# Last layer of a four-layer image kernel: both images stacked in the operand rows of the transforms

## The chip, the cores and the metric

The kernel runs on one core of one Trainium2 chip. The metric is the device time of one execution in microseconds.

## The reference

An activation of shape (2, 96, 48, 48) (two images, 96 channels) goes through four layers; each computes its result from the group-normalised x and adds it to x. The change is in the last one:

```python
x_0, x_05, x_1 = x[:, :32], x[:, 32:64], x[:, 64:]          # 32 channels each
x_0   = 3x3 convolution of x_0, weights gated per image
Fre   = Fh @ fftshift(x_05) @ Fw                            # fractional Fourier matrices, complex, per image
Mix   = gated 1x1 convolution of [Fre.real, Fre.imag]       # 64 -> 64, per image, plus bias
IFRFT = abs(Fh(-alpha) @ complex(Mix) @ Fw(-alpha)) / (H * W)
fre   = rfft2(x_1)
mix   = gated 1x1 convolution of [fre.real, fre.imag]       # 64 -> 64, per image, plus bias
x_1   = irfft2(complex(mix))
out   = 3x3 convolution of concatenate([x_0, IFRFT, x_1]) + bias
x     = x + out
```

H = W = 48; an rfft row has UH = 25 values. A fractional matrix is E diag(phase) E^T, with a real E of 48x48 and a phase that depends on the image's alpha.

## The kernel before, in words

The program is a list of blocks, one after another; a block ends when all five engines have met. The last layer (`l3`) is `group_norm`, `l3_gates`, `l3_forward`, `l3_inverse`. TensorE (PE) computes `lhsT^T @ rhs` from SBUF into one of eight PSUM banks; ScalarE (ACT) or VectorE (DVE) copies a bank out; SyncE (SP) issues every DMA; GpSimd (POOL) only clears tiles. An f32 matmul of the program is two PE instructions in the trace.

`l3_gates` computes the gates and the mixing weights `wg`, and loads `xh` (the image rows on 48 partitions), the tables, and `G0`, the shifted input of the first convolution.

`l3_forward` has four phases on TensorE, each a list of jobs of one PSUM bank; ACT copies every bank out (L1753, L1755), and a phase waits for the copies of the one before.
1. Rows (`rows_jobs`): for each of the BC = 64 image-channel pairs one matmul with the 48x48 `xh` of that pair as the stationary operand, 48 moving columns (`ef`) for the fractional part and 96 (`fh`) for the Fourier part. Result: `A1`, `A2` on 48 partitions.
2. Columns (`cols_jobs`): for each of the 48 rows j one matmul of `A1[:, :, j]` (48 rows, 64 weight columns) by `ef`, and two by `fw`, 50 columns each. Result on the 64 pairs: `Xh`, `Fz`. DVE multiplies `Xh` by the phases into `Zr` and `Zi`.
3. Fractional mixing (`frac_jobs`): per chunk of ten rows (FCH, five chunks) and per result (real, imaginary) three accumulating matmuls of 480 columns: `wg` of the real part, of the imaginary part (64 rows each), and a one-row matmul with the bias.
4. Fourier mixing (`mix_jobs`): the same with chunks of 250 columns.

```python
yield ([(wg[:, 0, 0, q, :], Zr[:, lo:hi, :].rearrange("p j k -> p (j k)"), 0, o, True, False),
        (wg[:, 0, 1, q, :], Zi[:, lo:hi, :].rearrange("p j k -> p (j k)"), 0, o, False, False),
        (bw[:, 0, q, :], e11[:, lo * H:hi * H], 0, o, False, True)], BC,
```

DVE turns the mixed values by the phases again (L1779 to L1783), and SP stores them to DRAM as `V` (L1670) and the Fourier part as `M` (L1672).

`l3_inverse` loads `Mu` and `Vj` from DRAM with the row index on 48 partitions (L1852, L1857). TensorE does the first convolution (`conv0_jobs`, 96 rows, 32 output rows), then kind 1 and 2 (inverse Fourier, `Mu` by `ih`, `A4` by `iw`) into `F`, then kind 3 and 4 (`Vj` by `ei`, `A3` by `ei`, squared by ACT). DVE adds the squares into `P2`, ACT takes the root. SP carries `F` and `P2` through DRAM into `cat`, channels on partitions (L1859 to L1870): `F` while kind 3 and 4 run, `P2` per image. The last convolution (L1912, nine taps of 384 columns, twelve banks) waits for `F` and, per image, for that image's `P2`. The order of the queues is the order of the statements in each engine's function.

## Time and profile before

| | us |
|---|---|
| median of 3 runs | 3371.29 (3369.62 to 3373.77) |
| profiled execution, its own time | 3376.56 |
| its span in the trace | 3374.7 |
| last layer from its gates to the end | 3003.3 to 3374.7 |
| forward block | 3034.9 to 3183.6 |
| inverse block up to the last convolution | 3183.6 to 3293.0 |
| last convolution | 3293.0 to 3366.4 |
| PE busy in the whole span | 67% |
| mean granted clock of TensorE | 0.853 |

In a table by stage each row is a stretch of the span: how long each engine was busy in it and with how many instructions, and the clock that TensorE was granted, as a share of 2.4 GHz (0.50 is 1.2 GHz). A group of instructions gives the busy time, the mean duration of one (for PE with its latency, so that instructions overlap), and the idle time before them. L12 is line 12 of the kernel; the lines of the changed kernel are its own.

### The profile page before, as it was taken

The page shows a single profiled execution, that of the slowest core. Times are in us where ns is not written, and L with a number is a line of the kernel's source. Part 1 is how long each engine was busy: PE and PEld are TensorE (multiplying, and loading weights), DVE is VectorE, ACT ScalarE, POOL GpSimd, SP SyncE. Part 2 cuts the span into 40 slices and gives each one's busy share as a digit, 9 for nine tenths or more (in the row PEclk, how much of TensorE's full clock was granted, in tenths as well). Part 3 has the DMA queues.
Part 4 walks back from the last instruction along what each step waited for, and adds up shares of the span by engine and source line. Part 5 has one row for each costly group of instructions (what it writes and reads, how often), then busy time and mean ns, then how long its engine had stood idle before and what let it go on. Part 6 is the DMA issues. An engine that isn't in the chain of part 4 may idle for free. (4 is left out here: it accounts for less than half of the span.)

```text
span 3374.7 us, 25934 instructions
## 1 busy us (share of the span) xinstructions
PE 2266.1 (67%) x7808; PEld 1113.2 (33%) x7808; DVE 2652.9 (79%) x2063; ACT 1636.3 (48%) x2346; POOL 2126.1 (63%) x1108
## 2 busy tenths in 40 slices
PE   4554466666666666666666664885079886939998
PEld 1221133233332332323223231322034443517294
DVE  7676799999999999999999997669556668952101
ACT  4454577767677767766777673253100006502130
POOL 4165799999999999999999995045300006910000
PEclk8766799999999999999999998766589898965659
DMA  1176434333443443433344335000387951040411
GB/s 42 59 219 216 132 121 128 120 111 121 133 122 114 117 127 123 127 113 123 122 127 122 109 124 201 35 0 0 91 301 264 322 205 37 12 59 1 47 19 32
DMA packets 156204, 387.94 MB, mean 115 GB/s; under 512 B 56883, under 2 KB 65367, under 8 KB 142647
## 3 DMA queue, kind: packets, MB, share of 16 engines
q1 hardware_dynamic: 150342, 368.07, 36.0%
q10 hardware_dynamic: 5730, 18.29, 1.5%
q8 instruction: 61, 1.00, 0.1%
q14 instruction: 71, 0.58, 0.1%
HBM read 311.32 MB, written 61.61 MB: 111 GB/s over the span
## 5 line engine op out<-in xcount | busy, mean ns | idle before, releaser
L811 POOL TENSOR_TENSOR l0c_r<-l0c_r,l0c_v 128x768 f32<-128x768 f32 x576 | 1041.0, 1823 | 23.7 <-DVE l0c_r L774 22.6
L839 ACT ACTIVATE ps<-l0c_dlt,l0c_na 128x512 f32<-128x512 f32 (+1 forms) x1152 | 625.9, 575 | 515.8 <-DVE l0c_h L800 492.0
L800 DVE TENSOR_TENSOR_SCAN l0c_h<-ps,l0c_h,l0c_r 128x768 f32<-128x768 f32 x384 | 703.4, 1832 | 5.0 <-issue 5.0
L820 POOL TENSOR_TENSOR l0c_hcp<-l0c_cb,l0c_h 128x768 f32<-128x768 f32 x384 | 699.8, 1822 | 0.6 <-DVE l0c_h L800 0.6
L864 ACT ACTIVATE l0c_r<-l0c_S,l0c_floor,l0c_na 128x768 f32<-128x768 f32 x576 | 583.6, 1014 | 14.2 <-ACT l0c_y L832 14.2
L704 PE MATMUL ps<-l0c_Bp,l0c_sel 96*128 96x512 bf16 (+1 forms) x1152 | 294.2, 338 | 439.2 <-DVE l0c_hcv L781 258.7
L737 PE MATMUL ps<-l0c_hcp,net_ident 128*128 128x512 f32 (+1 forms) x1536 | 582.8, 503 | 9.0 <-ACT l0c_y L832 6.0
L774 DVE SCALAR_TENSOR_TENSOR l0c_r<-l0c_r,ps 128x768 f32<-128x768 f32 x576 | 547.6, 951 | 6.4 <-PE ps L704 3.8
L737 PEld LDWEIGHTS ps<-l0c_hcp,net_ident 128*128 128x128 f32 x1536 | 270.3, 196 | 256.2 <-issue 199.3
L1297 PE MATMUL ps<-l_prod,l_wa 128*96 128x384 f32 (+1 forms) x888 | 292.1, 493 | 88.7 <-DVE l_prod L1281 88.7
L800 DVE TENSOR_TENSOR_SCAN l0c_h<-ps,l0c_r 128x768 f32<-128x768 f32 x192 | 339.4, 1768 | 0.0
L1281 DVE TENSOR_TENSOR l_prod<-l_base,l_other 128x2304 f32<-128x2304 f32 (+1 forms) x74 | 189.3, 2558 | 141.3 <-PE ps L1297 88.9
L737 PE MATMUL ps<-l0c_hcv,net_ident 128*128 128x512 f32 (+1 forms) x768 | 289.8, 500 | 1.1
L704 PEld LDWEIGHTS ps<-l0c_Bp,l0c_sel 96*128 96x128 bf16 x1152 | 85.7, 98 | 618.5 <-DVE l0c_r L774 529.0
L1378 POOL MEMSET l2g_pad<- 96x224 f32 x4 | 1.1, 281 | 363.0 <-POOLq L116 363.0
L1297 PEld LDWEIGHTS ps<-l_prod,l_wa 128*96 128x96 f32 (+1 forms) x888 | 146.7, 165 | 233.6 <-issue 144.2
L704 PE MATMUL ps<-l0c_Cp,l0c_sel 96*128 96x256 bf16 (+1 forms) x384 | 96.1, 332 | 157.8 <-DVE l0c_r L774 156.2
L162 ACT ACTIVATE net_rstd<-gn_t 96x2 f32<-96x2 f32 x4 | 0.8, 203 | 413.2 <-DVE gn_t L141 413.2
L1187 POOL TENSOR_TENSOR l_Z<-l_Z,l0f_prod 128x2304 f32<-128x2304 f32 x13 | 85.1, 6556 | 183.3 <-ACT l0f_prod L1108 182.7
L781 DVE TENSOR_TENSOR l0c_hcv<-ps,l0c_h 128x768 f32<-128x768 f32 x192 | 186.6, 972 | 0.0
L1493 PE MATMUL ps<-l_rows,l_diag 128*128 128x384 f32 x450 | 153.7, 504 | 34.8 <-ACT l_diag L1399 19.3
L737 PEld LDWEIGHTS ps<-l0c_hcv,net_ident 128*128 128x128 f32 x768 | 134.4, 195 | 124.4 <-issue 98.6
(261 smaller groups left out, 2821.6 us busy)
## 6 DMA issues: line engine op xcount, KB each, us to landing
l0c_cb<-cf SPq DMA_DIRECT2D x768, 192.0 KB, 3.4
l_other<-po SPq DMA_DIRECT2D x72, 1152.0 KB, 5.2
dlt<-l0s_dl SPq DMA_DIRECT2D x36, 384.0 KB, 3.5
v<-l0s_vv SPq DMA_DIRECT2D x36, 384.0 KB, 2.3
...
```

The costliest lines, as they stand in the source:

```text
L704: mm = pe.matmul(ps[:, lo:hi], sel[:, t % 2, n * 128:(n + 1) * 128], rows[:, i, lo - at:hi - at], start=True, stop=True)
L737: mm = pe.matmul(ps[:, lo:hi], ident[:, :], hc[:, lo - PY:hi - PY], start=(n == 0), stop=(n == N - 1))
L774: dve.scalar_tensor_tensor(rj, rj, 1.0, b_all, ALU.add, ALU.mult).then_inc(s_ub, 1)
L781: dve.tensor_tensor(hcv[:, dve_steps(j) % NHV, :], c_all, h[:, j % N, :], ALU.mult).then_inc(s_hv, 1)
L800: dve.tensor_tensor_scan(h[:, n, :], da[j % 2], r[:, j % NR, :], init, ALU.mult, ALU.add).then_inc(s_scan, 1)
L811: pool.tensor_tensor(r[:, j % NR, :], r[:, j % NR, :], v[:, (j // N) % 2, :], ALU.mult).then_inc(s_w, 1)
L820: pool.tensor_tensor(hcp[:, p % NHP, :], cb[:, p % NCB, :], h[:, e % N, :], ALU.mult).then_inc(s_hp, 1)
L839: act.activation(da[e % 2][:, part], dlt[:, i, part], ACT.Exp, scale=na[:, i, n:n + 1]).then_inc(done, 1)
L864: act.activation(r[:, j % NR, :], S[:, i, :], ACT.Tanh, bias=floor[:, :], scale=na[:, i, N + n:N + n + 1]).then_inc(s_tanh, 1)
L1281: dve.tensor_tensor(prod[0:n, s, :], base[0:n, s, :], other[0:n, s, :], ALU.mult).then_inc(s_prod, 1)
L1297: mm = pe.matmul(ps[0:C, c * BANK:c * BANK + CH], wa[0:height[i], i, :], prod[0:height[i], i % 3, c * CH:(c + 1) * CH], start=(i == 0), st ...
L1493: mm = pe.matmul(ps[:, o:o + CH], diag[:, tl, i, :], rows[:, tl, dy + 8 * c:dy + 8 * c + 8, dx:dx + W], start=(i == 0), stop=(i == NPE - 1))
```

## The change

Both images, or the real and the imaginary part, share one matmul:
- `xh` holds both images on 96 partitions. The row tables are block matrices: `ef2` is `ef` twice on the diagonal (96x96), `fh2` 96x192. One matmul per channel gives both images, side by side in the columns.
- `A1` and `A2` have 128 partitions; POOL clears them and the upper 80 stay zero; `ef` and `fw` are padded with zero rows to 128. The column matmuls are issued twice (q = 0, 1), into the lower and the upper 64 rows of a bank: the upper half repeats the real columns for the fractional part, and for the Fourier part the lower half gets the real 25 and the upper half the imaginary 25 columns. So the real and imaginary parts are stacked on 128 partitions.
- The phases are taken by DVE: `PZ`, `PA`, `PB` are 128x2304 tables computed at the block's start (three passes each). DVE reads the real columns from PSUM, multiplies by `PZ` into `Z`; after the mixing it reads two banks, multiplies them by `PA` and `PB`, adds, and SP stores that chunk of `V`.
- Mixing is one matmul of 128 rows with `wg` (real and imaginary results as 128 columns), a second with `ws` (the same weights, swapped and negated) for the turned product, each with a one-row matmul for the bias in the fractional part; in the Fourier part the bias goes into ACT's copy. Chunks there are of 20 rows (500 columns).
- The inverse does the first convolution, then the fractional part (`Vj`, `A3` by `ei2`, a block matrix), then the Fourier part (`Mu` by `ih2`, copied out by DVE, then `A4` by `iw2`), each with both images in 96 or 100 rows. `P2` and `F` have 96 partitions.
- SP loads `V` before `M`, in four gathers each. It then sends `P2` in two halves of 16 channels and `F` in four chunks of 8, each by a store to DRAM, a wait for its landing and two gathers into `cat`; the last convolution waits for all of them.
- POOL clears only the borders of `G0` and `cat`.

```diff
+            for name in ("ef2", "fh2", "ef", "fw"):
+                sp.dma_start(tr[name][tuple(slice(None) for _ in tr[name].shape)], a[name]).then_inc(s_tr, 16)
...
+            pool.memset(tr["A1"][:, :, :, :], 0.0).then_inc(s_pad, 1)
+            pool.memset(tr["A2"][:, :, :, :, :], 0.0).then_inc(s_pad, 1)
...
+            for p, b, rows in groups:
+                step(dve.tensor_tensor(wg[rows, :, :, b, :], gate[rows, :, :].rearrange("p f (q o) -> p f q o", q=2),
+                                       wt[rows, :, :].rearrange("p f (q o) -> p f q o", q=2), ALU.mult))
...
+            step(dve.tensor_scalar(ws[:, 0, :, :], wg[:, 0, 1, :, :], -1.0, None, ALU.mult))
+            step(dve.tensor_scalar(ws[:, 1, :, :], wg[:, 0, 0, :, :], 1.0, None, ALU.mult))
...
+            for i, (lo, hi) in enumerate(FCH):
                 sp.wait_ge(s_v, i + 1)
-                sp.dma_start(d["V"][:, i, :, :], M[:, i, :, :]).then_inc(s_out, 16)
-            sp.wait_ge(s_m, 1)
-            sp.dma_start(d["M"].rearrange("p u i k -> p (u i k)"), Mz[:, :, :, :].rearrange("p u i k -> p (u i k)")
-                         ).then_inc(s_mst, 16)
+                sp.dma_start(d["V"][:, lo:hi, :], V[:, lo:hi, :]).then_inc(s_vst, 16)
...
-            for lo, hi in FCH:
-                yield ([(A1[:, :, j], ef[:, :], (j - lo) * H, H, True, True) for j in range(lo, hi)], BC,
...
-                    mms.append((A2[:, :, 0, u], fw[:, 0, :], (u - lo) * 2 * UH, 2 * UH, True, False))
-                    mms.append((A2[:, :, 1, u], fw[:, 1, :], (u - lo) * 2 * UH, 2 * UH, False, True))
...
-                    yield ([(wg[:, 0, 0, q, :], Zr[:, lo:hi, :].rearrange("p j k -> p (j k)"), 0, o, True, False),
-                            (wg[:, 0, 1, q, :], Zi[:, lo:hi, :].rearrange("p j k -> p (j k)"), 0, o, False, False),
-                            (bw[:, 0, q, :], e11[:, lo * H:hi * H], 0, o, False, True)], BC,
...
+            for i, (lo, hi) in enumerate(R0):
+                free(q_r0 + i)
+                for c in range(lo, hi):
+                    o = (q_r0 + i) % 8 * BANK + (c - lo) * 2 * H
+                    mm = pe.matmul(ps[0:W, o:o + 2 * H], xh[:, 0, c, :], ef2[:, :], start=True, stop=True)
+                mm.then_inc(s_mm, 1)
...
+                    mm = pe.matmul(ps[0:W, o:o + 4 * H], xh[:, 1, c, :], fh2[:, :], start=True, stop=True)
...
+            for i, (lo, hi) in enumerate(FCH):
+                free(q_c0 + i)
+                for j in range(lo, hi):
+                    o = (q_c0 + i) % 8 * BANK + (j - lo) * H
+                    for q in range(2):
+                        mm = pe.matmul(ps[BC * q:BC * q + BC, o:o + H], A1[:, :, :, j].rearrange("p b c -> p (b c)"),
+                                       ef[:, :], start=True, stop=True)
+                mm.then_inc(s_mm, 1)
...
+                for u in range(lo, hi):
+                    o = (q_c1 + i) % 8 * BANK + (u - lo) * UH
+                    for q in range(2):
+                        for s in range(2):
+                            mm = pe.matmul(ps[BC * q:BC * q + BC, o:o + UH],
+                                           A2[:, :, :, s, u].rearrange("p b c -> p (b c)"),
+                                           fw[:, s, UH * q:UH * q + UH], start=(s == 0), stop=(s == 1))
...
+                for w, b, q in ((wg[:, 0, :, :, :], bw, q_fr + 2 * i), (ws[:, :, :, :], bws, q_fr + 2 * i + 1)):
+                    free(q)
+                    pe.matmul(ps[:, bank(q, n)], w.rearrange("p q b o -> p (q b o)"),
+                              Z[:, lo:hi, :].rearrange("p j k -> p (j k)"), start=True, stop=False)
+                    pe.matmul(ps[:, bank(q, n)], b[:, :, :].rearrange("p q n -> p (q n)"), e11[:, lo * H:hi * H],
+                              start=False, stop=True).then_inc(s_mm, 1)
...
+                pe.matmul(ps[:, bank(q_mx + i, (hi - lo) * UH)], wg[:, 1, :, :, :].rearrange("p q b o -> p (q b o)"),
+                          Fz[:, lo:hi, :].rearrange("p u k -> p (u k)"), start=True, stop=True).then_inc(s_mm, 1)
...
+            phase(PZ, csz, 1, ALU.subtract)
+            phase(PA, cs, 1, ALU.subtract)
...
+                dve.scalar_tensor_tensor(Z[:, lo:hi, :].rearrange("p j k -> p (j k)"),
+                                         ps[:, bank(q_c0 + i, (hi - lo) * H)], float(H),
+                                         PZ[:, lo:hi, :].rearrange("p j k -> p (j k)"), ALU.mult, ALU.mult
+                                         ).then_inc(s_ed, 1)
+            phase(PB, cs, 0, ALU.add)
...
+                for k, (dst, P, done) in enumerate(((v1, PA, s_m1), (v2, PB, s_m2))):
+                    q = q_fr + 2 * i + k
+                    dve.wait_ge(s_mm, q + 1)
+                    dve.tensor_tensor(dst[:, s, 0:n], ps[:, bank(q, n)], P[:, lo:hi, :].rearrange("p j k -> p (j k)"),
+                                      ALU.mult).then_inc(s_ed, 1)
+                dve.wait_ge(s_ed, evac_count(q_fr + 2 * i + 1))
+                dve.tensor_tensor(V[:, lo:hi, :].rearrange("p j k -> p (j k)"), v1[:, s, 0:n], v2[:, s, 0:n], ALU.add
...
+                    sp.dma_start(Vj[H * b:H * b + H, :, s, :], d["V"][o:o + C3, :, :].rearrange("c j k -> j c k")
+                                 ).then_inc(s_V, 16)
...
-            sp.wait_ge(s_ev, first[3])
-            sp.dma_start(d["o"][1], F[:, :, :]).then_inc(s_fst, 16)
-            sp.wait_ge(s_edge, 1)
-            sp.wait_ge(s_fst, 16)
             for b in range(B):
-                sp.dma_start(interior(cat[2 * C3:C, b, :, :]),
-                             d["o"][1, :, C3 * b:C3 * b + C3, :].rearrange("h c w -> c h w")).then_inc(s_cf, 16)
-            for b in range(B):
-                rows = slice(C3 * b, C3 * b + C3)
-                sp.wait_ge(s_root, b + 1)
-                sp.dma_start(d["o"][0][:, rows, :], P2[:, rows, :]).then_inc(s_pst, 16)
-                sp.wait_ge(s_pst, 16 * (b + 1))
-                sp.dma_start(interior(cat[C3:2 * C3, b, :, :]),
-                             d["o"][0, :, rows, :].rearrange("h c w -> c h w")).then_inc(s_cp[b], 16)
...
+            def to_cat(i, lo, hi):
+                for b in range(B):
+                    r0 = C3 * (2 if i else 1)
+                    sp.dma_start(interior(cat[r0 + lo:r0 + hi, b, :, :]),
+                                 d["o"][i, H * b:H * b + H, lo:hi, :].rearrange("h c w -> c h w")).then_inc(s_cat, 16)
+
+            for g in range(2):
+                lo, hi = HALF * g, HALF * (g + 1)
+                sp.wait_ge(s_root, g + 1)
+                sp.dma_start(d["o"][0, :, lo:hi, :], P2[:, lo:hi, :]).then_inc(s_pst, 16)
+                sp.wait_ge(s_pst, 16 * (g + 1))
+                to_cat(0, lo, hi)
+            for i, (lo, hi) in enumerate(K2):
+                sp.wait_ge(s_ea, evac_count(q_2 + i))
+                sp.dma_start(d["o"][1, :, 2 * lo:2 * hi, :], F[:, 2 * lo:2 * hi, :]).then_inc(s_fst, 16)
+                sp.wait_ge(s_fst, 16 * (i + 1))
+                to_cat(1, 2 * lo, 2 * hi)
...
+                    mm = pe.matmul(ps[0:D2, o:o + D2], Vj[:, c, :, :].rearrange("p q k -> p (q k)"), ei2[:, :],
+                                   start=True, stop=True)
...
+                    mm = pe.matmul(ps[0:D2, o:o + D2], A3[:, c, :], ei2[:, :], start=True, stop=True)
...
+                    mm = pe.matmul(ps[0:Q2, o:o + 2 * D2], Mu[:, 2 * c:2 * c + 2, :, :].rearrange("p c q k -> p (c q k)"),
+                                   ih2[:, :], start=True, stop=True)
...
+                        mm = pe.matmul(ps[0:D2, o:o + 2 * W], A4[:, c, s, :], iw2[:, s, :],
+                                       start=(s == 0), stop=(s == 1))
...
+            pe.wait_ge(s_cat, 16 * B * (2 + len(K2)))
...
+    def blocks(m):
+
+        r, n = m.shape
+        two = np.zeros((2, r, 2, n), f)
+        two[0, :, 0], two[1, :, 1] = m, m
+        return two.reshape(2 * r, 2 * n)
```

How the queues are changed, at three places. First TensorE in the forward block, before (`ps` is PSUM, `l3w_xbuf` is `xh`, `l3f_A` is `A1` and `A2`; the figures are output rows by moving columns; one row is one matmul of the program):

```order
L1737 MATMUL ps<-l3w_ef,l3w_xbuf 48x48 x64
L1737 MATMUL ps<-l3w_fh,l3w_xbuf 48x96 x64
L1737 MATMUL ps<-l3w_ef,l3f_A 64x48 x48
L1737 MATMUL ps<-l3w_fw,l3f_A 64x50 x96
L1737 MATMUL ps<-l3f_Zr,l3w_wg 64x480
L1737 MATMUL ps<-l3f_Zi,l3w_wg 64x480
L1737 MATMUL ps<-l3f_e,l3w_bw 64x480
```

and now:

```order
L1722 MATMUL ps<-l3w_ef,l3w_xh 48x96 x32
L1728 MATMUL ps<-l3w_fh,l3w_xh 48x192 x32
L1736 MATMUL ps<-l3w_ef,l3w_A 64x48 x96
L1746 MATMUL ps<-l3w_fw,l3w_A 64x25 x192
L1756 MATMUL ps<-l3f_Z,l3w_wg 128x480
L1758 MATMUL ps<-l3f_e,l3w_bw 128x480
L1756 MATMUL ps<-l3f_Z,l3w_ws 128x480
L1758 MATMUL ps<-l3f_e,l3w_bws 128x480
```

The 64 row matmuls of either kind became 32 with twice the columns, the column matmuls 96 of 48 and 192 of 25 columns, and the mixing has two matmuls per result in place of three.

Second, TensorE in the inverse block before:

```order
L1901 MATMUL ps<-l_G,l_w0g 32x384 x36
L1901 MATMUL ps<-l3i_ih,l3i_Mu 50x96 x64
L1901 MATMUL ps<-l3i_iw,l3i_A 48x48 x128
L1901 MATMUL ps<-l3i_ei,l3i_Vj 48x48 x128
L1901 MATMUL ps<-l3i_ei,l3i_A 48x48 x128
L1912 MATMUL ps<-l3i_cat,l3i_w 96x384 x108
```

and now:

```order
L1935 MATMUL ps<-l_G,l_w0g 32x384 x36
L1944 MATMUL ps<-l3i_ei,l3i_Vj 96x96 x32
L1952 MATMUL ps<-l3i_ei,l3i_A 96x96 x32
L1959 MATMUL ps<-l3i_ih,l3i_Mu 100x192 x16
L1968 MATMUL ps<-l3i_iw,l3i_A 96x96 x32
L1977 MATMUL ps<-l3i_cat,l3i_w 96x384 x108
```

The fractional stages moved ahead of the Fourier stages, and each of the four has a quarter of the matmuls, of twice the width.

Third, SyncE in the inverse block behind the loads, before (`o` is the scratch in DRAM):

```order
L1859 DMA o<-l3i_F 48x3072
L1863 DMA l3i_cat<-o 32x48x48 x2
L1868 DMA o<-l3i_P 48x1536
L1870 DMA l3i_cat<-o 32x48x48
L1868 DMA o<-l3i_P 48x1536
L1870 DMA l3i_cat<-o 32x48x48
```

and now, the first three of six such trips:

```order
L1904 DMA o<-l3i_P 96x768
L1898 DMA l3i_cat<-o 16x48x48 x2
L1904 DMA o<-l3i_P 96x768
L1898 DMA l3i_cat<-o 16x48x48 x2
L1909 DMA o<-l3i_F 96x384
L1898 DMA l3i_cat<-o 8x48x48 x2
```

What was one trip for `F`, issued ahead of everything, and one per image for `P2` is now two trips for `P2` and then four for `F` in one queue.

## Rows read from the trace of the kernel before

**Rows 1.** Chain of waits, 2880 to 3375 us: start, us, what.
```profile
by line: PE ps L1901 21.3%; PE ps L1912 14.6%; issue 0.6%; ACT l3i_A L1937 0.2%; DVE net_X L1955 0.1%
...
3290.34 2.70 issue
3293.04 72.47 PE ps L1912 x216
```

**Rows 2.** By stage: length; busy us (instructions) per engine; granted clock; DMA share, GB/s.
```profile
core 0: us, PE busy (x) PEld busy (x) DVE busy (x) ACT busy (x) POOL busy (x), PEclk, DMA share, GB/s
3003.30:3034.90 31.60, 6.47 (x42) 2.68 (x42) 4.29 (x22) 4.38 (x9) 4.09 (x1) 0.50 1.07 138
3034.90:3045.80 10.90, 10.19 (x127) 10.19 (x128) 10.59 (x6) 3.08 (x6) 0.00 (x0) 0.50 0.02 4
3045.80:3067.10 21.30, 20.76 (x132) 20.44 (x130) 5.05 (x2) 7.64 (x15) 0.00 (x0) 0.50 0.00 1
3067.10:3077.70 10.60, 10.57 (x96) 10.58 (x97) 0.00 (x0) 2.26 (x4) 0.00 (x0) 0.50 0.00 0
3077.70:3099.70 22.00, 21.49 (x195) 21.32 (x193) 5.02 (x2) 3.23 (x6) 0.00 (x0) 0.50 0.01 1
3099.70:3150.20 50.50, 49.88 (x60) 10.19 (x60) 0.01 (x1) 5.37 (x11) 0.00 (x0) 0.50 0.00 0
3150.20:3178.50 28.30, 27.80 (x60) 10.12 (x60) 15.21 (x6) 3.67 (x11) 0.00 (x0) 0.50 0.20 42
3178.50:3183.60 5.10, 0.00 (x0) 0.00 (x0) 0.00 (x0) 0.10 (x1) 0.00 (x0) 0.50 0.57 120
```

**Rows 3.** The same, around changes of clock, and in an earlier layer.
```profile
3183.60:3189.00 5.40, 5.33 (x9) 1.60 (x10) 0.00 (x0) 0.57 (x1) 4.26 (x1) 0.50 0.90 91
3189.00:3209.60 20.60, 20.60 (x64) 6.82 (x62) 0.00 (x0) 5.75 (x10) 0.00 (x0) 1.00 1.00 82
3209.60:3212.90 3.30, 3.30 (x41) 3.28 (x41) 0.00 (x0) 2.27 (x4) 0.00 (x0) 1.00 0.02 5
3212.90:3293.00 80.10, 76.29 (x859) 75.65 (x857) 3.50 (x2) 26.66 (x46) 0.00 (x0) 0.50 0.15 23
3293.00:3298.20 5.20, 5.16 (x8) 2.38 (x9) 0.00 (x0) 1.16 (x1) 0.00 (x0) 0.50 0.26 57
...
2184.00:2232.00 48.00, 44.33 (x58) 14.39 (x57) 32.51 (x27) 16.03 (x21) 0.00 (x0) 0.50 0.00 1
```

**Rows 4.** Groups of PE matmuls, one line: busy us, mean ns | idle before.
```profile
L222 PE MATMUL ps<-l0x_XG,l0p_w_in 96*128 96x384 f32 x48 | 21.2, 603 | 11.4 <-DMA l0p_cb<-in_cb 7.8 <-ACT l0p_pad L240 3.7
...
L222 PE MATMUL ps<-l0x_XG,l0p_w_in 96*64 96x384 f32 x48 | 12.1, 663 | 12.8 <-ACT l_Z L238 12.8
```

**Rows 5.** Groups of ACT and DVE.
```profile
L1755 ACT COPY l3f_A<-ps 48x480 f32<-48x480 f32 x18 | 9.9, 552 | 35.2 <-PE ps L1737 35.2
...
L1768 DVE TENSOR_TENSOR l3f_Zi<-l3w_cs 64x2304 f32<-64x2304 f32 x1 | 2.6, 2551 | 0.0
...
L774 DVE SCALAR_TENSOR_TENSOR l0c_r<-l0c_r,ps 128x768 f32<-128x768 f32 x576 | 547.6, 951 | 6.4 <-PE ps L704 3.8
...
L1923 ACT ACTIVATE l3i_P<-l3i_P 48x1536 f32<-48x1536 f32 x2 | 3.0, 1483 | 1.8 <-DVE l3i_P L1948 1.8
...
L1923 ACT ACT_TABLE_LOAD x1 | 1.3, 1283 | 0.0
```

**Rows 6.** SyncE: an issue, landings of L1857, landings by tile (KB, median us).
```profile
3253.98 0.99 SPq L1863 DMA_DIRECT2D l3i_cat<-o  x2
...
DMA to landing us min/median/max: 11.1/13.3/15.6
...
l3i_cat<-o SPq DMA_DIRECT2D x4, 288.0 KB, 3.9
...
o<-l3i_F SPq DMA_DIRECT2D x1, 576.0 KB, 5.0
o<-l3i_P SPq DMA_DIRECT2D x2, 288.0 KB, 3.1
...
l_back<-l_acc SPq DMA_DIRECT2D x1, 144.0 KB, 2.4
```

More of the change, by code:

```diff
@@ new lines, in l3_inverse, with by_dve, evac_count, bank @@
+        q_3 = B * NC
+        q_4 = q_3 + len(K3)
+        q_1 = q_4 + len(K3)
+        q_2 = q_1 + len(K1)
+        q_c = q_2 + len(K2)
+        HALF = C3 // 2
+        half_done = [next(i for i, (lo, hi) in enumerate(K3) if hi >= HALF * (g + 1)) for g in range(2)]
+        def by_dve(q):
+            return q_1 <= q < q_2
+        def evac_count(q):
+            return sum(by_dve(i) == by_dve(q) for i in range(q + 1))
+        def bank(q, n):
+            return slice(q % 8 * BANK, q % 8 * BANK + n)
@@ L1905, in _ @@
[L1905 to L1916 removed]
+                    pe.wait_ge(s_ed if by_dve(q - 8) else s_ea, evac_count(q - 8))
@@ L1918, in _ @@
+            for n in range(B * NC):
+                b, c = divmod(n, NC)
+                free(q_c + n)
+                for i in range(TAPS):
+                    dy, dx = divmod(i, 3)
+                    mm = pe.matmul(ps[0:C, bank(q_c + n, CH)], w2[:, i, :],
+                                   cat[:, b, dy + 8 * c:dy + 8 * c + 8, dx:dx + W], start=(i == 0),
+                                   stop=(i == TAPS - 1))
+                mm.then_inc(s_c2, 1)
         @block.scalar
         def _(act):
-            def root(b):
-                rows = slice(C3 * b, C3 * b + C3)
-                act.wait_ge(s_sum, b + 1)
-                act.activation(P2[:, rows, :], P2[:, rows, :], ACT.Sqrt, scale=1.0 / (H * W)).then_inc(s_root, 1)
```

541 lines of the change are left out of this document (265 added, 276 removed).

## The prediction

> **What bounds the kernel now.** I read the page's chain of waits first: its last stretch is PE alone, lines L1901 and L1912, with almost no other engine [rows 1]. So in the last layer TensorE's own time is the path. The table by stage then shows which part of that is what: from 3034.9 to 3178.5 us the forward block keeps PE busy all through [rows 2], and of the inverse the same holds (76 of 80 us [rows 3]). The reader is to see two things in it. The stages cost what their streamed columns cost (10.9, 21.3, 10.6, 22.0, 50.5 and 28.3 us), and the granted clock is 0.50 in every one, which is the 1.2 GHz level. The third view is the clock around the changes of shape [rows 3]. The first convolution (L1901 on l_G, operands of 96 rows) starts at 0.50 and is at 1.00 (2.4 GHz) 5.4 us later; it holds that for 20.6 us. Then the 48-row stage begins, still at 1.00, and 3.3 us later the clock is 0.50 and stays there for 80 us although PE is busy 76 of them. The last convolution, 96 rows again, is at 1.00 after 5.2 us. In a much earlier layer 48 us of almost full PE, on alternating operands of 128, 64 and 2 rows, ran at 0.50. What went before each rise was therefore continuous work of 96 or more rows, what went before the fall was continuous work of 48. This is what the change can move: it brings nearly every operand to 96, 100 or 128 rows.
>
> The profiled execution took 3376.56 us (span 3374.7), 5.3 above the median of 3371.29. I make the sum in the trace's times and take it from the median. About 0.2% (7 us) is what a measurement of this kernel can tell from no change.
>
> **Forward block, before 148.7 us** (3034.9 to 3183.6) [rows 2]. An f32 matmul of the program is two PE instructions in the trace; their price goes by the streamed columns.
> - Row transforms (L1722, L1728). 32 + 32 matmuls of 96 and 192 columns replace 64 + 64 of 48 and 96: the same columns, so at 1.2 GHz the same 10.2 + 20.8 = 31.0 us. The gain is the clock: as in the convolutions I let it rise 5.4 us after the start, and the rest runs at half the price: 5.4 + 25.6/2 = 18.2 us. ACT's copies are 7 of 480 columns at 0.55 us [rows 5] and 16 of 384 at less, under PE's 0.8 and 0.65 us for such a bank at 2.4 GHz.
> - Real columns (L1736). 96 matmuls of 48 columns where 48 were, each twice for the lower and the upper 64 rows of PSUM. Such halves are in the trace: L222's 48 instructions into 128 rows took 21.2 us, its 48 into 64 rows, in pairs, 12.1 [rows 4]. A pair costs what one costs. So 10.6 us at 1.2 GHz, 5.3 at 2.4; I take 6.0, and 0.6 for the hand-over behind the last copy.
> - Complex columns (L1746). 192 matmuls of 25 columns where 96 of 50 were, in such pairs: 192 pairs of instructions. Before, an instruction there cost 112 ns (21.5 us over 192), hardly more than the 110 of the 48-column ones (10.57 over 96) and far from the 80 of 48 columns with 48 weights (10.2 over 127): the 64 weight columns set it, and they stay. So 21.5 us at 1.2 GHz, 10.8 at 2.4. No row shows what clock a stage gets whose loads outlast its streams at 128 rows. The bounds are the two prices. The row nearest in shape is this stage's own predecessor (50 columns under 64 weights, at 0.50); the stages that held 1.00 at 96 rows stream 384 columns a load. So I take that the clock falls, about 5 us in (it took 3.3 to 5.4 us in [rows 3]): 5 + (21.5 - 10) = 16.5 us, and 0.6 for the hand-over.
> - Fractional mixing (L1756, L1758). Per chunk and result one matmul of 128 rows and one of one row (the bias), 20 in place of 30: 49.88 x 40/60 = 33.3 us at 1.2 GHz, 16.6 at 2.4. With the clock down when it starts, and every second matmul of one row, the nearest row is the mixed one of the earlier layer, which stayed at 0.50 [rows 3]. I take 33.3.
> - Fourier mixing (L1763). 3 matmuls (500, 500 and 200 columns) in place of 30. An instruction of 480 columns or so cost 0.83 us (49.88/60), or 1.73 ns a column: 2 x 1200 x 1.73 = 4.2 us instead of 28.3. The bias goes into ACT's copy, free.
> - End: ACT's copy 0.6, then M's store as now, 5.0 from issue to the next block [rows 2, 6].
> - VectorE, which waited here most of the time, now takes TensorE's results out of PSUM. Six passes of 2.55 us [rows 5] and three small ones end 16.3 us in, before the first real column bank (about 20). The third phase (7.7 us) ends near 34 us, while the mixing's first bank comes after 42. Three operations per chunk at under 0.95 us (that is what 768 elements from PSUM took [rows 5]) stand against 6.6 us of PE. Costed at nothing, with complex columns and mixing as their cover; if PE were at 2.4 GHz throughout, 2.9 against 3.3 still fits.
>
> Sum: 0.2 + 18.2 + 6.0 + 0.6 + 16.5 + 0.6 + 33.3 + 4.2 + 5.6 = 85.2 us, a gain of 63.5.
>
> **Gates block.** Two larger tables ride in a block that ends with its transfers: +0.5 us. GpSimd's clears of A1 and A2, 9216 elements, I cost at nothing: it was busy 4.09 of the block's 31.6 us, with 4800 [rows 2].
>
> **Inverse block, before 109.4 us to the last convolution** (3183.6 to 3293.0) [rows 1].
> - First convolution: unchanged, 26.0 us, ends at 2.4 GHz.
> - The fractional stages (L1944, L1952) come next: 32 + 32 matmuls of 96 columns and 96 rows in place of 128 + 128 of 48. 128 instructions at 82 ns (some 40 took 3.30 us at 2.4 GHz with 96 columns [rows 3]) are 10.5 us, plus 0.7 of hand-overs, where 42 stood. The V they need comes first on the queue now: 6144 pieces of 192 bytes. Before, M's 3072 pieces and V's 6144 were all in about 21 us after the block began (the last gather landed 15.6 us after its issue at 3189.5 [rows 6]), so 6144 need some 15 of the 26 us.
> - M now has 6144 pieces of 100 bytes behind them: in by about 30 us, needed at 37. If that cover fails, only the F chunks wait, which have slack (below).
> - Squares, the sum, the table load (1.3) and half a root (1.48/2 [rows 5], I take 0.9): the first half is ready at 26.0 + 11.2 + 2.9 = 40.1 us. The Fourier stages (L1959: 32 instructions of 192 columns, L1968: 64 of 96) take 5.2 + 5.3 us at 2.4 GHz, end near 48, and are hidden.
> - What is late next is the SyncE queue. All six round trips through DRAM stand in a row before the last convolution, where one of 7.0 us (store 3.1, gather 3.9) stood and the rest was under other work. A round is a store, its landing (3.1 us for 288 KB [rows 6]) and two gather issues (0.99 us [rows 6]); the next store waits for the store alone. Two rounds of P at 4.0; four of F (144 KB; 2.4 landed such a load, 3.1 the double size) at 3.6; the last gather, 72 KB, lands in 2.8 (bounds 2.4, that load, and 3.9, the gathers of 288 KB). 40.1 + 8.0 + 14.4 + 2.8 = 65.3 us. Gain 44.1.
> - The last convolution starts from 1.2 GHz as it does now, 73.4 us, no change.
>
> Sum of all: -63.5 - 44.1 + 0.5 = -107.1: **3371.3 - 107.1 = 3264.2 us.**
>
> **Rivals.**
> 1. *The clock also survives the complex columns.* For it: the operands have all 128 rows, and once risen it held through everything of 96 rows. Against: short streams, and mixing with one-row matmuls. Then the complex columns take 12.0, fractional mixing 16.7, Fourier mixing 2.1: 4.5 + 16.6 + 2.1 less, 3241 us. Chance 0.30.
> 2. *The clock does not answer to rows.* The stages then cost their columns at 1.2 GHz: forward 31.0 + 10.6 + 21.5 + 33.3 + 4.2 and 7.0 of hand-overs and end = 107.6 us, gain 41.1; the fractional stages 20.5, so the six rounds start 10 us later: gain 34.1. With the gates' 0.5 together -74.7, so 3297 us. Against it stand the fall and the two rises [rows 3]. The Trainium skill ("TensorE: Matmul & The Clock Gate", Part 1: The HAM clock gate) makes the clock depend on whether TensorE is kept busy and says nothing of rows; by that rule stacking would leave the clock as it is. The trace does not agree with busy time alone: the 48- and 64-row stages were busy without a break at 0.50. Chance 0.10.
> 3. *Halves do not pair* where each needs its own weights loaded, L222's being much longer streams. Real columns 12 and complex 38 us: +27.5, 3292 us. Chance 0.06.
> 4. *The rounds are dearer,* 7 us each, as P's full trip to its landing was: 40.1 + 42 in place of 65.3, +17, 3281 us. Chance 0.08.
> 5. *Slower.* The same six rounds, at the place between the first root and the last convolution. Below 22 us a round they cannot eat the rest of the gain (40.1 + 6 x 22 = 172 = 109.4 + 63); from there on the kernel is slower, at 25 us it is 3389. The longest gather of this trace, 15.6, with F's store, 5.0 [rows 6], makes 20.6, but that gather had 3072 pieces behind 3072 others, and a round's have 768 at most. Chance 0.03.
>
> **How the numbers follow.** The forecast case has 0.42 and its own range is 3254 to 3275; a last 0.01 is no effect at all. The range runs from below rival 1 to above rival 4, 3234 to 3287, and leaves rivals 2, 3 and 5 out. Only rival 5 and the last case are not faster: 0.96, 0.01, 0.03.
>
> **What would show it.** Clock at 1.00 from about 5 us into L1722; L1746 near 16 us with the fall inside it; L1756/L1758 near 33 us; L1763 near 4; L1944 and L1952 some 5 us each at 1.00; a gap of about 17 us of idle PE before L1977 with SyncE's gathers in it. A clock of 0.50 in L1728, an L1736 above 11 us, or a gap over 25 us would make the prediction wrong, each in its own term.

## The result, and the profile after the change

The changed kernel took 3288.22 us (median of 4 runs, 3280.86 to 3293.45), the kernel before beside it 3372.36 (3369.62 to 3373.77): a ratio of 0.975, interval 0.9735 to 0.977. It is faster by 84 us. 107 were forecast (3264.2, range 3234 to 3287), so the median lies 24.0 us above the forecast and 1.2 us above the range. Repeated later beside the experiments, the changed kernel took 3291.1 us; the two medians differ by 2.9 us, single runs of the first four by up to 12.6.

The profiled execution took 3293.45 us (span 3291.6). The table by stage of the changed kernel, with the columns of [rows 2], one row per stage in the order of the forecast's terms:

```profile
core 0: us, PE busy (x) PEld busy (x) DVE busy (x) ACT busy (x) POOL busy (x), PEclk, DMA share, GB/s
3003.00:3032.40 29.40, 5.70 (x46) 1.88 (x47) 7.06 (x26) 4.23 (x8) 8.58 (x5) 0.50 1.06 153
3032.40:3050.50 18.10, 18.09 (x126) 15.68 (x127) 15.92 (x9) 10.23 (x22) 0.00 (x0) 0.84 0.01 2
3050.50:3061.50 11.00, 11.00 (x196) 10.97 (x194) 2.63 (x4) 0.85 (x2) 0.00 (x0) 0.87 0.01 1
3061.50:3085.00 23.50, 23.50 (x388) 23.47 (x385) 8.14 (x4) 1.15 (x2) 0.00 (x0) 0.57 0.01 2
3085.00:3121.70 36.70, 36.70 (x43) 10.02 (x41) 8.45 (x13) 0.33 (x1) 0.00 (x0) 0.50 0.07 27
3121.70:3130.80 9.10, 4.34 (x7) 1.82 (x6) 1.11 (x2) 1.77 (x3) 0.00 (x0) 0.50 0.23 90
3130.80:3157.30 26.50, 26.43 (x73) 8.52 (x73) 0.00 (x0) 6.31 (x11) 0.56 (x2) 0.88 0.87 88
3157.30:3168.20 10.90, 10.90 (x129) 10.90 (x129) 0.95 (x1) 7.06 (x14) 0.00 (x0) 1.00 0.01 2
3168.20:3179.00 10.80, 10.80 (x99) 10.66 (x97) 5.00 (x9) 4.95 (x8) 0.00 (x0) 1.00 0.59 79
3179.00:3209.40 30.40, 0.04 (x2) 0.01 (x1) 0.00 (x0) 0.47 (x1) 0.00 (x0) 0.54 0.47 50
3209.40:3283.50 74.10, 72.97 (x216) 36.23 (x216) 7.36 (x12) 0.00 (x0) 0.00 (x0) 0.96 0.00 0
```

Beside [rows 2] and [rows 3] the reader sees what the change brought. The row transforms are down from 32.2 us to 18.1. The first convolution of the inverse block and its four transform stages are 48.2 us (3130.8 to 3179.0) where they were 106.7 (3183.6 to 3290.3). The Fourier mixing and the end of the forward block are 9.1 us where they were 33.4. Not brought is a higher clock in the complex columns and the fractional mixing (0.57 and 0.50). New is the tenth row: 30.4 us in which TensorE does nothing and the DMA engines are 47% busy. In [rows 1] 2.70 us stood in that place.

Inside the forward block the timeline of TensorE (start, length, group) shows what one instruction costs:

```profile
3050.86 10.87 PE L1736 MATMUL ps<-l3w_ef,l3w_A 128*64 128x48 f32 x190
3061.52 23.57 PE L1746 MATMUL ps<-l3w_fw,l3w_A 128*64 128x25 f32 x384
```

Of the same view, the beginning of the fractional mixing:

```profile
3085.02 1.97 PE L1756 MATMUL ps<-l3f_Z,l3w_wg 128*128 128x480 f32 x2
3086.92 1.96 PE L1758 MATMUL ps<-l3f_e,l3w_bw 1*128 1x480 f32 x2
```

And the clock over the two column stages, in the columns of the table above:

```profile
3050.50:3058.60 8.10, 8.10 (x145) 8.07 (x144) 1.97 (x3) 0.85 (x2) 0.00 (x0) 1.00 0.01 2
3058.60:3062.00 3.40, 3.40 (x63) 3.40 (x62) 0.88 (x2) 0.00 (x0) 0.00 (x0) 0.50 0.00 0
3062.00:3065.40 3.40, 3.40 (x61) 3.40 (x60) 3.37 (x3) 0.00 (x0) 0.00 (x0) 1.00 0.02 5
```

The real columns' 192 instructions took 11.0 us from their first start to that of the next line: 57 ns each, 114 for the pair of halves. The clock was at 1.00 for the first 8.1 us of that and at 0.50 for the rest, and the instructions started as often at either: one every 56 ns (by the start times in the trace). The complex columns' 384 took 23.5 us, 122 ns a pair; the clock came back at 3062.0 and fell for good at 3065.4, and again the instructions took as long in between as afterwards (60 and 61 ns). In the mixing a matmul, two instructions, takes 1.90 us.

The chain of waits of the changed kernel behind the first root (start, us, what):

```profile
3171.10 2.54 DMA o<-l3i_P
...
3174.57 6.52 DMA o<-l3i_P
...
3182.03 4.89 DMA o<-l3i_F
...
3187.70 4.69 DMA o<-l3i_F
...
3193.15 5.13 DMA o<-l3i_F
...
3199.05 4.92 DMA o<-l3i_F
...
3204.29 5.05 DMA l3i_cat<-o
```

Six stores stand in the chain one behind the other. The first lands in 2.54 us, all others in 4.7 to 6.5, although four of them carry half as much. So the time that is missing has two places, about 13 us each: the forward block (98.4 us for 85.2) and the rounds through DRAM (38.3 for 25.2).

### The profile page after: what moved, and what is told of

It is laid out like the page before. It is cut to its first block and busy times, and to the rows that moved or that the text cites. A ratio compares the mean times of both kernels' runs of the same rounds, so it can differ in the third digit from the quotient of the medians.

```text
span 3291.6 us, 24792 instructions
## 1 busy us (share of the span) xinstructions
PE 2159.3 (66%) x7226; PEld 1034.3 (31%) x7226; DVE 2659.7 (81%) x2092; ACT 1607.6 (49%) x2295; POOL 2126.9 (65%) x1113
## 5 line engine op out<-in xcount | busy, mean ns | idle before, releaser
L800 DVE TENSOR_TENSOR_SCAN l0c_h<-ps,l0c_h,l0c_r 128x768 f32<-128x768 f32 x384 | 693.2, 1805 | 5.0 <-issue 5.0
L774 DVE SCALAR_TENSOR_TENSOR l0c_r<-l0c_r,ps 128x768 f32<-128x768 f32 x576 | 533.1, 925 | 6.8 <-PE ps L704 4.1
```

Source lines behind the costliest of these rows:

```text
L774: dve.scalar_tensor_tensor(rj, rj, 1.0, b_all, ALU.add, ALU.mult).then_inc(s_ub, 1)
L800: dve.tensor_tensor_scan(h[:, n, :], da[j % 2], r[:, j % NR, :], init, ALU.mult, ALU.add).then_inc(s_scan, 1)
```

## The experiments

Times are medians; "changed" is the changed kernel, 3288 to 3291 us.

### Rows alone

The whole change rests on the belief that the clock answers to rows. This is the kernel before, with nothing but zero rows:

```diff
-        Vj = sb("Vj", [H, BC, 2, H])
...
+        R = 96
+        Vj = sb("Vj", [R, BC, 2, H])
...
+            for t in (ih[:, :], iw[:, :, :], Mu[:, :, :], ei[:, :], Vj[:, :, :, :], A4[:, :, :, :], A3[:, :, :, :]):
+                pool.memset(t, 0.0).then_inc(s_z, 1)
```

> The kernel BEFORE with one thing of the change alone: the tiles that the inverse transforms read (Vj, Mu, ei, ih, iw, A3, A4) get zero rows up to 96 partitions, filled by POOL, and the instructions keep their number and columns. Theory (rows raise the clock): the four transform stages, which run at a granted clock of 0.5 before, run at 1.0 after their first few us, their instructions fall to about half, and the block ends some 25 to 38 us earlier, so the median falls to about 3335 to 3346 us. Rival (the clock does not answer to rows, the gain of the change is that it has fewer instructions): the stages stay at 0.5 and the time is within 3 us of before's 3372, or a few us above it by the fills.

3340.3 us against 3372.7, ratio 0.991 (0.989 to 0.9925). TensorE's timeline of the transform stages, the same 896 instructions as before:

```profile
3204.65 10.76 PE L1908 MATMUL ps<-l3i_ih,l3i_Mu 96*50 96x96 f32 x128
3215.98 11.72 PE L1908 MATMUL ps<-l3i_iw,l3i_A 96*48 96x48 f32 x256 [0.57 <-ACT l3i_A L1946]
3227.54 11.68 PE L1908 MATMUL ps<-l3i_ei,l3i_Vj 96*48 96x48 f32 x256
3239.80 11.72 PE L1908 MATMUL ps<-l3i_ei,l3i_A 96*48 96x48 f32 x256 [0.57 <-ACT l3i_A L1946]
```

and the clock over them (table by stage):

```profile
3204.00:3256.00 52.00, 46.37 (x899) 45.29 (x897) 3.50 (x2) 29.69 (x50) 0.00 (x0) 0.99 0.27 40
```

Before, these stages ran from 3209.6 to 3290.3, 80.7 us, nearly all at 0.50 [rows 1, 3]. Here they run from 3204.7 to 3251.6, 46.9 us, at 0.99. The columns, the instructions and the results are the same; only empty rows were added, and GpSimd's filling of them, which ends at 3202.0 under the first convolution. The theory holds, and the rival (no answer to rows) falls. Both operands got the rows, so which of the two counts is not shown. By the rule of the Trainium skill ("TensorE: Matmul & The Clock Gate", Part 1: The HAM clock gate), that the clock follows how busy TensorE has been, both kernels should have had the same clock, since by the profile they are about equally busy there. The trace does not agree with it in that form: 76 busy us of 80 at 0.50 before, 46 of 52 at 0.99 here.

### The bias matmuls of one row

```diff
-            bw, bws = sb1("bw", [1, 2, BC]), sb1("bws", [1, 2, BC])
+            bw, bws = sb1("bw", [128, 2, BC]), sb1("bws", [128, 2, BC])
...
-        e11 = sb("e11", [1, H * H])
+        e11 = sb("e11", [128, H * H])
```

> The changed kernel with the bias matmuls of the fractional mixing on 128 rows instead of one (bw, bws and e11 get 127 zero rows). Theory (the one-row matmuls between the 128-row ones hold the clock down): the granted clock rises a few us into the mixing, the stretch falls from 36.7 us to 19 to 24 us, and the kernel by 12 to 18 us. Rival A (only the change of weights between 128 rows and one row costs, 136 ns at each switch, 36 of them): the clock stays at 0.5, the stretch falls by about 5 us to 32. Rival B (neither): 36.7 us, no change.

3267.8 us, 20 to 23 below the changed kernel, more than the 12 to 18 expected. Timeline of the mixing (lines are shifted by 8: L1764 is the matmul on Z, L1766 the bias):

```profile
3090.37 1.80 PE L1766 MATMUL ps<-l3f_e,l3w_bw 128*128 128x480 f32 x2
3091.97 1.59 PE L1764 MATMUL ps<-l3f_Z,l3w_ws 128*128 128x480 f32 x2
3093.40 0.97 PE L1766 MATMUL ps<-l3f_e,l3w_bws 128*128 128x480 f32 x2
3094.21 0.97 PE L1764 MATMUL ps<-l3f_Z,l3w_wg 128*128 128x480 f32 x2
```

The mixing starts at 0.50 as before; from 3093.2 on, 4.6 us in, the clock is at 1.00 and a matmul's 1.60 us become 0.81. The stretch ends at 3106.45: 17.8 us instead of 36.7, and 2.2 instead of 4.3 for the Fourier mixing. The theory holds for the larger part, and the price of switching that rival A took for all of it is the smaller part. At 0.50 a matmul among others of 128 rows takes 1.60 us (3090.37 to 3091.97), where those that alternate between 128 rows and one took 1.90. That is 0.3 us for each of 20, some 6 of the 19 us; the rest is the clock.

### Where the weights lie

```diff
-                  "A1": sb1("A1", [128, B, C3, H]), "A2": sb1("A2", [128, B, C3, 2, H])}
+                  "A1": sb1("A1", [128, H, B, C3]), "A2": sb1("A2", [128, 2, H, B, C3])}
...
-                        mm = pe.matmul(ps[BC * q:BC * q + BC, o:o + H], A1[:, :, :, j].rearrange("p b c -> p (b c)"),
+                        mm = pe.matmul(ps[BC * q:BC * q + BC, o:o + H], A1[:, j, :, :].rearrange("p b c -> p (b c)"),
```

> The changed kernel with the weights of the column transforms of the forward block adjacent in memory (A1 and A2 laid out with the 64 columns of one instruction side by side, where they were 192 and 384 bytes apart); ScalarE's copies write with a stride instead. Theory (the strided read of the weights has a rate of its own, whatever the granted clock): at a clock of 1.0 a pair of instructions falls from 114 ns to about 60, the real columns from 11.0 to 6 to 7 us, the complex ones from 23.5 to 13 to 20 us, the latter by where the clock falls; the kernel 4 to 14 us faster, less what ScalarE's strided writes cost. Rival (the two halves' weight loads go one after the other at a fixed rate): a pair stays at 110 to 114 ns at 1.0, no change of time.

3265.9 us, 22 to 25 below the changed kernel, more than the 4 to 14 expected. Timeline of TensorE:

```profile
3052.31 5.75 PE L1736 MATMUL ps<-l3w_ef,l3w_A 128*64 128x48 f32 x190
3057.90 11.39 PE L1746 MATMUL ps<-l3w_fw,l3w_A 128*64 128x25 f32 x384
3069.21 1.07 PE L1756 MATMUL ps<-l3f_Z,l3w_wg 128*128 128x480 f32 x2
3070.22 1.07 PE L1758 MATMUL ps<-l3f_e,l3w_bw 1*128 1x480 f32 x2
```

and where the clock falls:

```profile
3077.21 1.60 PE L1756 MATMUL ps<-l3f_Z,l3w_wg 128*128 128x480 f32 x2
3078.74 1.96 PE L1758 MATMUL ps<-l3f_e,l3w_bw 1*128 1x480 f32 x2
```

The real columns' last 190 instructions now take 5.6 us (59 ns a pair instead of 114), the complex ones' 384 take 11.3 (59 instead of 122). And the clock no longer falls in them: it stays at 1.00 until 3077.6, through both column stages and 8.4 us of the mixing, which therefore ends 29.1 us after its start instead of 36.7. This is why the expected figure was too low: it let the clock fall within the complex columns and gave the mixing nothing. The columns bring 17.3 us and the mixing 7.5. So 128 rows alone do not hold the clock; with the strided weights it fell in the same instructions. At 1.00 the alternating rows of the mixing still cost: 1.00 us a matmul against 0.81 where all have 128.

The companion run asks whether the two halves get in each other's way. It leaves out the instructions of the upper half:

```diff
-                    for q in range(2):
+                    for q in range(1):
```

> The changed kernel with only one of the two copies of the real column transform: the instructions for output rows 64 to 127 (the copy that the imaginary part is made of) are left out, the upper rows of Z are zero, so V's values are not the reference's. 96 instructions instead of 192 in this stage. Theory (the strided read of the weights sets the pace): one instruction takes about as long as the pair did, 105 to 114 ns at 1.0, and the stage stays at 10 to 11 us. Rival (the halves' loads go one after the other, 55 ns each): 55 to 60 ns for one instruction, the stage falls to 5.3 to 6 us.

```profile
3044.29 10.72 PE L1736 MATMUL ps<-l3w_ef,l3w_A 128*64 128x48 f32 x96
```

96 instructions take 10.5 us to the start of the next line, 110 ns each; 192 took 11.0. Leaving half of them out saves 0.5 us, so the halves do pair (rival 3 of the prediction falls). With the run before, which changed only where the weights lie, this says what a pair waits for: the read of 64 weights that lie 192 bytes apart, about 110 ns. It was 110 at 0.50 in the kernel before (10.57 us for 96 [rows 2]) and is 111 at 1.00 and at 0.50 in the changed kernel: this load does not follow TensorE's clock. The kernel's single run took 3284.5 us.

### The rounds through DRAM

Six rounds cost 38.3 us where 25.2 were forecast. First edit: the stores leave SyncE's queue.

```diff
-                sp.wait_ge(s_ea, evac_count(q_2 + i))
-                sp.dma_start(d["o"][1, :, 2 * lo:2 * hi, :], F[:, 2 * lo:2 * hi, :]).then_inc(s_fst, 16)
...
+                act.wait_ge(s_ea, evac_count(q_2 + i))
+                act.dma_start(d["o"][1, :, 2 * lo:2 * hi, :], F[:, 2 * lo:2 * hi, :]).then_inc(s_fst[i], 16)
```

> The changed kernel with the six stores of P and F issued by ScalarE, each right behind the copy or root that makes it ready and on ScalarE's own queue; SyncE keeps only the twelve gathers. Theory (a store stands on SyncE's queue behind the gathers of the round before, so that a round costs 5.4 to 7.5 us instead of the 4 us that were forecast): the stores land 2 to 4 us after they are issued, all by about 3184, the last gathers end 10 to 16 us earlier, the idle stretch of TensorE before the last convolution falls from 30.4 us to 15 to 20, and the kernel by 10 to 16 us. Rival (the DMA engines themselves are full with the small pieces: they are busy 48% of the 30 us, with gathers and stores of 192 bytes a piece): the stores take longer in their turn and the idle stretch stays above 26 us.

3278.4 us, 10 to 13 below the changed kernel; the idle stretch is 18.6 us. DMA issues with their landing (KB, median us), ScalarE's queue is ACTq:

```profile
o<-l3i_P ACTq DMA_DIRECT2D x2, 288.0 KB, 2.7
l3i_cat<-o SPq DMA_DIRECT2D x4, 144.0 KB
o<-l3i_F ACTq DMA_DIRECT2D x4, 144.0 KB, 6.3
```

The size is as expected and the reason is not. A store of F, alone on a queue of its own, still takes 6.3 us (the first one 7.4: issued at 3174.75, landed at 3182.10), while P's, with nothing ahead, take 2.7. So it does not wait on SyncE's queue. What stands ahead of it are the gathers' small pieces at the DMA engines. The four stores now do this wait together: issued 1.4 us apart, they land within 1.5 us (3182.10 to 3183.58), and that is the gain. Both readings had a part of it: theory in the time, rival in the cause.

Second edit: one round for F.

```diff
-            for i, (lo, hi) in enumerate(K2):
...
-                sp.dma_start(d["o"][1, :, 2 * lo:2 * hi, :], F[:, 2 * lo:2 * hi, :]).then_inc(s_fst, 16)
...
+            sp.dma_start(d["o"][1, :, :, :], F[:, :, :]).then_inc(s_fst, 16)
```

> The changed kernel with F stored and gathered in one round (576 KB, then two gathers) instead of four. Theory (the fixed part of a round, the wait for the gathers ahead and the landing, is what the four cost): the one store is issued at 3182, lands at about 3190, its gathers end at about 3199, the idle stretch falls by 8 to 12 us to 18 to 22. Rival (rounds cost by their bytes): 30 us as now, or more, since no gather can begin before the whole of F has landed.

3271.6 us (3271.3 to 3272.1), 17 to 19 below the changed kernel; the idle stretch is 14.3 us, better than the 18 to 22 expected. SyncE's queue:

```profile
3176.22 0.52 SPq L1908 DMA_DIRECT2D o<-l3i_F  x1
3181.96 1.08 SPq L1898 DMA_DIRECT2D l3i_cat<-o  x2
```

and the stretch of these last gathers (by stage), beside that of the eight small ones of the run before:

```profile
3182.00:3188.00 6.00, 0.08 (x1) 0.08 (x1) 0.00 (x0) 0.00 (x0) 0.00 (x0) 0.50 0.87 98
```

```profile
3182.10:3196.90 14.80, 0.00 (x0) 0.00 (x0) 0.00 (x0) 0.00 (x0) 0.00 (x0) 0.50 0.61 47
```

The two gathers of all F, 3072 pieces, were in by 3187.9, 5.9 us after their issue. The eight gathers of 8 channels, the same 3072 pieces, took 14.8 us at half the rate (47 GB/s for 98) with the engines less busy (0.61 for 0.87). That asks for a cause in the shape of a gather. Third edit, more rounds:

```diff
+                for k in range(2):
+                    c = 2 * lo + 4 * k
+                    sp.dma_start(d["o"][1, :, c:c + 4, :], F[:, c:c + 4, :]).then_inc(s_fst, 16)
...
```

> The changed kernel with each of the four rounds of F cut in two, 72 KB stored and two gathers of four channels each time; bytes and pieces in all as before. Theory (a round has a price that hardly depends on what it carries, since gathers of fewer channels move their 192-byte pieces more slowly): each of the four added rounds costs 4 to 5.5 us, the idle stretch of TensorE grows from 30.4 to 46 to 52 us and the kernel by 16 to 22. Rival (rounds cost by their bytes): the idle stretch grows by less than 6 us.

3308.5 us, 17 to 20 above the changed kernel; the idle stretch is 52.0 us, both as the theory has it. Stores of F on SyncE's queue:

```profile
3192.32 0.38 SPq L1911 DMA_DIRECT2D o<-l3i_F  x1
...
3197.90 0.38 SPq L1911 DMA_DIRECT2D o<-l3i_F  x1
```

5.5 us from round to round with half the bytes: the price of a round does not go by its bytes. Last edit, the same bytes and pieces, cut by image:

```diff
-                sp.dma_start(d["o"][1, :, 2 * lo:2 * hi, :], F[:, 2 * lo:2 * hi, :]).then_inc(s_fst, 16)
...
-                to_cat(1, 2 * lo, 2 * hi)
...
+                g, b = divmod(i, B)
+                rows, lo, hi = slice(H * b, H * b + H), HALF * g, HALF * (g + 1)
...
+                sp.dma_start(d["o"][1, rows, lo:hi, :], F[rows, lo:hi, :]).then_inc(s_fst, 16)
...
+                sp.dma_start(interior(cat[2 * C3 + lo:2 * C3 + hi, b, :, :]),
+                             d["o"][1, rows, lo:hi, :].rearrange("h c w -> c h w")).then_inc(s_cat, 16)
```

> The changed kernel with the four rounds of F cut another way: each stores and gathers 16 channels of one image (144 KB, one gather of 768 pieces) instead of 8 channels of both (144 KB, two gathers of 384 pieces). Bytes, pieces and stores per round are the same. Theory (a gather is dealt out by its channels, so 8 channels use 8 of the 16 DMA engines and 4 use 4, which is why a gather of 4, 8 or 16 channels takes about as long: 48 pieces an engine): with 16 engines for the same 768 pieces a round falls from 5.4 to 5.9 us to about 4, the idle stretch from 30.4 to 22 to 26 us, the kernel by 5 to 8 us. Rival (a round has a fixed price that has nothing to do with the share of the engines): only the second gather's issue goes, 0.3 us a round, under 2 us in all.

3278.8 us (3276.0 to 3284.3), 9 to 12 below the changed kernel, a little more than the 5 to 8 expected; the idle stretch is 22.6 us, as expected. SyncE's queue:

```profile
3183.43 0.52 SPq L1911 DMA_DIRECT2D o<-l3i_F  x1
...
3187.14 0.52 SPq L1911 DMA_DIRECT2D o<-l3i_F  x1
...
3190.89 0.52 SPq L1911 DMA_DIRECT2D o<-l3i_F  x1
```

A round with 144 KB and 768 pieces is now 3.7 us. The rival (a fixed price) falls. Gathers of 4, 8 and 16 channels spread over 4, 8 and 16 DMA engines, and a store that touches all 16 then waits for the laden ones. The completions in the trace say the same: of the changed kernel's second store of F eight came at 3189.4 to 3189.6 and eight at 3192.0 to 3192.4; with gathers of 4 channels, twelve at 3188.4 to 3188.6 and four at 3191.5 to 3191.6. The Trainium skill ("DMA: Bandwidth & Descriptors", Why a DMA increments its semaphore by 16 and not by 1) states this rule: the number of engines is the largest up to 16 that divides the slowest dimension of both sides. The trace agrees, with the 8 and the 4 above.

### The idle stretch filled, and all together

```diff
-        q_3 = B * NC
+        EARLY = 6
+        q_3 = EARLY
...
+            first_conv(True)
+            pe.wait_ge(s_ea, evac_count(q_c - 1))
             pe.wait_ge(s_cat, 16 * B * (2 + len(K2)))
```

> The changed kernel with the second half of the inverse block's first convolution (6 of 12 banks, 13 us of TensorE) behind the transform stages instead of ahead of them. Theory (the rounds of stores and gathers set the end of the idle stretch, and TensorE has nothing else to do in it): the first root is ready some 12 to 13 us earlier, every round with it, the half convolution runs within the former idle stretch, which falls from 30.4 to about 17 us, and the kernel by 11 to 13 us. Rival (the transforms then wait for the gathers of V and M, which land 12 and 20 us into the block, or the clock has not risen yet): 2 to 8 us.

3276.1 us, 12 to 15 below the changed kernel, as the theory has it; the last convolution waits 17.6 us. (Of the rival's kind the transforms wait 0.9 us for a load.)

```profile
L1987 PE MATMUL ps<-l3i_cat,l3i_w 96*96 96x384 f32 x216 | 73.0, 502 | 17.6 <-issue 17.6
```

> All together: adjacent weights, bias matmuls on 128 rows, stores on ScalarE's queue, half the first convolution behind the transforms. If the parts add up: 22 us (adjacent) and 20 us (bias rows), of which up to 7 us are the same microseconds of the mixing at the lower clock, then 10 to 16 and 11 to 13 us in the inverse block, where the last is bounded by the idle stretch of 30: the kernel 55 to 65 us below the changed one, 3223 to 3235 us. Rival (the rounds are bound by the DMA engines, so that the two edits of the inverse block give little more than one): 3240 to 3250 us.

3225.8 us, inside the expected 3223 to 3235; the last convolution waits 7.9 us. From 3039.7 us on the forward block now runs at 1.00 to its last matmul (by stage: the rest of the row transforms with both column stages, then the mixing):

```profile
3039.70:3068.90 29.20, 29.20 (x666) 26.73 (x664) 22.20 (x13) 15.00 (x38) 0.00 (x0) 1.00 0.01 3
3068.90:3086.40 17.50, 17.50 (x52) 8.69 (x48) 9.57 (x15) 1.00 (x2) 0.00 (x0) 1.00 0.15 56
```

The fractional and the Fourier mixing take 17.5 us together where the changed kernel needed 41. What is left is F's eight small gathers, so the last kernel keeps the four stores and gathers once:

```diff
-                to_cat(1, 2 * lo, 2 * hi)
...
+            to_cat(1, 0, C3)
```

> The four edits together (adjacent weights, bias matmuls on 128 rows, stores on ScalarE's queue, half the first convolution behind the transforms) and F's four stores followed by one pair of gathers of all 32 channels instead of four pairs of eight. Theory (the eight small gathers of F, from 3130.5 to 3147 in the run with eight, cost more than two whole ones, which took 5.9 us after one store): the idle stretch ahead of the last convolution falls from 7.9 us to 0 to 2 and the kernel from 3225.8 to 3217 to 3220 us. Rival (the time goes by the pieces, 3072 of 192 bytes either way): no change, 3224 to 3228.

3215.9 us (3213.2 to 3220.0), ratio to before 0.954 (0.953 to 0.955), slightly better than the 3217 to 3220 expected:

```profile
L1994 PE MATMUL ps<-l3i_cat,l3i_w 96*96 96x384 f32 x216 | 69.9, 485 | 0.9 <-ACT l3i_cat L2007 0.9
```

The last convolution waits 0.9 us, for ScalarE and no longer for a DMA. TensorE has no gap left of that kind, so the clock is still up when it starts: it takes 69.9 us where it took 73.0.

The repeat of the changed kernel:

> The changed kernel again, nothing edited, on the chip of the next two: its runs lay between 3280.9 and 3293.5 us, those of the kernel before within 4 us. Both readings: a median of 3283 to 3291. If the spread belongs to the program (at what moment the granted clock rises and falls within its stages differs from run to run), it is again 8 to 13 us; if it was the chip of that hour, 2 to 4 us.

3291.1 us (3288.4 to 3291.9). A spread of 3.5 us, not the 12.6 of the first four runs. So that spread is not shown to belong to the program; what it was stays open. In this trace the clock falls once, at 3056.6 in the real columns, and stays down until 3135.1, in the inverse block.

## Why the prediction was wrong

The forecast of the direction and of most of the gain held; the size was off in three terms of the sum. By its steps:

- **The clock answers to rows.** Right, though rows are not all of it (below). The rise came 5.7 us into the row transforms (3038.1) and 6.3 us into the inverse block (3137.1), and the zero rows showed it by themselves. Rival 2 (3297 us) lies only 9 us from the result, for other reasons: a time near a rival's is no evidence for it.
- **Row transforms** 18.2 us: 18.1. **Fourier mixing and end** 9.8: 9.1. **Gates** 32.1: 29.4, 2.7 better. The forecast added 0.5 for two larger tables, but the block's last transfer landed at 3031.9, before the change at 3034.4; why is not shown.
- **Real columns** 6.6 us: 11.0. **Complex columns** 17.1: 23.5. The failed step is the one that let these stages halve with the clock, "21.5 us at 1.2 GHz, 10.8 at 2.4". It had seen that the 64 weight columns set the price (112 and 110 against 80 ns) and still scaled the price by the clock. The read of strided weights keeps its 110 ns at either clock. The prediction's own prices at 1.2 GHz, 10.6 and 21.5 us, would nearly have met it; the remaining 2.0 us of the complex columns (a pair took 122 ns, an instruction before 112) are left, for which no run shows a reason. The pairing of the halves, which looked the bolder assumption, held.
- **The fall in the complex columns** about 5 us in: that the clock falls was right, the place was not. It fell 8.1 us into the real columns already (3058.6), came back for 3.4 us and fell again 3.9 us into the complex ones (3065.4). This cost nothing, since neither stage follows the clock. With adjacent weights the same instructions hold 1.00, and with bias matmuls of 128 rows the mixing does too: rival 1 (the clock survives) was two edits away.
- **Fractional mixing** 33.3 us: 36.7. The clock was right (0.50). The failed step is the average of 0.83 us an instruction, carried over from a stage in which one matmul in three followed one of like rows; now none does, and each alternation costs 0.3 us a matmul. The row of the earlier layer that the forecast took for the clock ([rows 3], from 2184 on) held this price too; two instructions of 128 rows alternate there with two of 64:

```profile
2190.34 41.97 PE L1046 MATMUL ps<-l_Y,l_c 128*128 128x384 f32 x53 [3.67 <-PEq L873]
```

  That is 0.79 us for 384 columns, and the mixing's instructions of 384 columns now start 0.79 us apart as well. At 0.83 us for 480 they had been counted as 0.66.
- **First root ready** 40.1 us into the inverse block: its store was issued at 40.3. The fractional pair of stages took 10.9 us (11.2 forecast) and the Fourier pair 10.8 (10.5), hidden behind P's rounds as forecast.
- **The rounds** 25.2 us: 38.3. The failed step is "the next store waits for the store alone". It waits at the engines for the gathers of the round before, and a gather of 8 channels loads 8 engines as heavily as one of 16 loads 16. By parts: P's rounds 3.5 and 7.5 us (8.0 forecast together), F's four 22.3 (14.4), the last gather 5.1 (2.8). The 3.6 us forecast for a round of F was the price with all 16: cut by image it was 3.7, and the idle stretch 7.8 us shorter. Rival 4 had the mechanism nearly (7 us each; only P's second round was so dear, F's were 5.2 to 5.9) and was given 0.08. The sign that the prediction named for this, a gap over 25 us, came: 30.4.
- **Last convolution** and what follows: 0.5 us more.

Sum: in the forward block -0.3 (hand-over and rows), +4.4, +6.4, +3.4 and -0.7 make +13.2; the gates -2.7, the inverse block +13.3, the last convolution and the end +0.5, and the gates' block began 0.3 us earlier. That is 24.0, the distance of the median from the forecast.

The range ended at 3287, above rival 4 alone: dearer columns and dearer rounds were each weighed as a rival of its own, a dearer mixing at the low clock not at all. Columns, mixing and rounds all came dearer together.
